# A graph kernel's second sort and sums: both chunks packed densely, items of two tiles, and ScalarE's source one-hots

## What is computed

```
agg  = jax.ops.segment_sum(x[nbr], dst, num_segments=n)      # here x is xn; "dst" is edge_index[0] = src
cnt  = jax.ops.segment_sum(jnp.ones((nbr.shape[0],), x.dtype), dst, num_segments=n)
mean = agg / jnp.maximum(cnt, 1.0)[:, None]
gnn  = x @ W1.T + b1 + mean @ W2.T + b2
...
x = x + gnn(xn) + mix(xn)          # mix: per head of 32, kv = k^T v / N with normalised k, v; out = q kv + xn
x = x + ffn(_layernorm(x))         # top-1 of 8 experts, capacity 977, 256 -> 1024 -> 256
```

## Time and profile before

| | us |
|---|---|
| median of 3 runs | 1998.8 (1995.85 to 1999.64) |
| the profiled execution's own time | 1998.75 |
| its span | 1997.1 |
| stage until the first gather | 305 |
| gathers of chunk one, 392 | 531.5 |
| gathers of chunk two, 438 | 577.4 |
| last gather to the end of the span | 583 |

### The profile page before, as it was taken

How to read it: one execution, slowest core, us unless ns; L and a number is a source line. 1 busy time by engine, 2 the same in 40 slices (tenths; PEclk the granted TensorE clock), 3 DMA queues, 4 the chain that set the end, 5 groups by cost and what they waited for, 6 DMA issues and landing times. The chain is left out here.

```text
span 1997.1 us, 27369 instructions
## 1 busy us (share of the span) xinstructions
PE 1529.7 (77%) x6558; PEld 885.3 (44%) x6558; DVE 1367.3 (68%) x3735; ACT 710.2 (36%) x1954; POOL 985.5 (49%) x969
## 2 busy tenths in 40 slices
PE   4599995667778777365665558798593999999997
PEld 2255542233333333133333335454482766666665
DVE  8998997889998988476666657666781433444344
ACT  4488890008787876000000002111281222222221
POOL 0000006777777777777777777777263111111111
PEclk7699997679999998555555558878655999999999
DMA  6980013333333333743333334444464123323200
GB/s 185 180 151 32 32 36 86 98 100 94 99 98 97 95 96 98 86 123 100 101 100 101 98 111 131 127 132 127 140 226 163 41 96 97 105 96 103 101 9 5
DMA packets 101500, 204.49 MB, mean 102 GB/s; under 512 B 19794, under 2 KB 64760, under 8 KB 99392
## 3 DMA queue, kind: packets, MB, share of 16 engines
q0 software_dynamic: 49488, 131.52, 23.6%
q1 hardware_dynamic: 43164, 64.16, 12.1%
q10 hardware_dynamic: 8700, 7.07, 1.2%
HBM read 157.43 MB, written 49.89 MB: 104 GB/s over the span
## 5 line engine op out<-in xcount | busy, mean ns | idle before, releaser
L511 POOL DMA_INDIRECT w<-xn_parts,idx x830 | 856.4, 1032 | 260.8 <-issue 236.4
L1018 DVE TENSOR_TENSOR XA<-XA,bank 128x257 f32 x878 | 367.3, 418 | 280.9 <-PE bank L765 250.1
L764 PE MATMUL bank<-w,S 128*128 (+1 forms) x878 | 294.0, 337 | 275.0 <-SPq L461 114.6
L764 PEld LDWEIGHTS bank<-w,S 128*128 128x128 f16 x878 | 93.4, 106 | 486.8 <-issue 301.1
L765 PE MATMUL bank<-w,S 128*128 (+1 forms) x878 | 298.2, 342 | 0.0
L1800 POOL DMA_INDIRECT out<-ob,tok x64 | 66.5, 1040 | 401.2 <-DVE ob L1786 384.9
L596 ACT ACTIVATE LV<-LH,v 125x128 f16<-125x128 f16 x600 | 182.5, 388 | 195.8 <-DVE LH L1268 195.5
L1724 PE MATMUL bank<-w,ht 128*117 128x256 f32 (+1 forms) x1024 | 223.7, 379 | 0.0
L1713 PE MATMUL bank<-xt,w 128*128 128x468 f32 (+1 forms) x512 | 214.8, 578 | 0.8 <-ACT xt L1738 0.8
L1748 ACT ACTIVATE ht<-bank,b1c 128x468 f32<-128x468 f32 (+1 forms) x128 | 85.6, 669 | 333.4 <-PE bank L1713 333.4
L1724 PEld LDWEIGHTS bank<-w,ht 128*117 128x117 f32 (+1 forms) x1024 | 188.8, 186 | 30.5 <-issue 0.4
(11 more groups left out here) (290 smaller groups left out, 2326.0 us busy)
## 6 DMA issues: line engine op xcount, KB each, us to landing
w<-f SPq DMA_DIRECT2D x16, 1024.0 KB, 7.6
w<-xn_parts,idx POOLq DMA_INDIRECT x830, 2.8
expert_rows<-XA SPq DMA_DIRECT2D x2, 6296.5 KB, 62.7
xb<-expert_rows SPq DMA_DIRECT2D x8, 1028.0 KB, 11.4
xb<-expert_rows SPq DMA_DIRECT2D x8, 939.7 KB
XA<-x SPq DMA_DIRECT2D x6, 1024.0 KB, 5.6
xn_parts<-w POOLq DMA_DIRECT2D x12, 512.0 KB, 3.3
work<-x ACTq DMA_DIRECT2D x48, 128.0 KB, 2.2
```

Of the source, the lines that this page charges most:

```text
L511: pool.indirect_dma_start(ring[:, o:o + 2 * D], None, tab, bass.IndirectOffsetOnAxis(ap=idx[:, t:t + 1], axis=0)).then_inc(s_g[t % RING], 16)
L764: pe.matmul(psA[t % AR][:, 0:AGW], lhs, ring_high[:, ds(o, AGW)], start=True, stop=True)
L1018: v.tensor_tensor(XA[:, ds(o, AGW)], XA[:, ds(o, AGW)], psA[t % AR][:, 0:AGW], ALU.add).then_inc(s_ev, 1)
```

## The change

1. **Chunk one becomes dense too.** Its 392 tiles become 344; `place` and `decode` go, `place_dense` and `decode_dense` serve both chunks. So the tile one-hots of chunk one are 344 wide instead of 392.
2. **An item is a pair of tiles and a block.** Two neighbouring tiles ("a two") are summed into one PSUM bank by four matmuls and added once. There are 172 and 219 twos, 220 and 267 items: 487 adds instead of 878, and 974 halves of items (each two matmuls) instead of 878 tiles.
3. **TensorE takes slots from registers in both chunks**, SyncE tells it of landed twos and lets twos go in both, and GpSimd waits for `s_free` in both.
4. **The steps are halves of items**: 440 in chunk one, 534 in chunk two. The side plan is spread over `STEPS0 - GR - SB` = 416 of 440. Heads and `own` keep their step numbers (`own` from step 288).
5. **ScalarE makes chunk two's `S`.** VectorE leaves the negated sources in 32-bit; ScalarE makes |iota - source| for 8 tiles (8 ACTIVATEs of 128) and then relu(1 - that) in one ACTIVATE of 1024, 67 times. Heads, `own` and the one-hots are interleaved on ScalarE. VectorE's 61 `source_onehots` of chunk two go; chunk one has 55 instead of 49.

```diff
-    for cols, padded in ((352, True), (448, False)):
-        tiles = (cols * EP + NB * (P - 1)) // P if padded else -(-cols * EP // P)
+    for cols in (352, 448):
+        tiles = -(-cols * EP // P)
...
+DENSE = tuple(-(-c[1] * EP // (2 * P)) * 2 for c in CHUNKS)
+TWOS = tuple(n // 2 for n in DENSE)
+ITEMS = tuple(n + NB - 1 for n in TWOS)
...
+STEPS0, STEPS1 = 2 * ITEMS[0], 2 * ITEMS[1]
...
-        while k < len(costs) and spent < total * (t + 1) // (T0 - RING):
+        while k < len(costs) and spent < total * (t + 1) // (STEPS0 - GR - SB):
...
+        for two in range(sum(TWOS)):
...
+            landed(two)
+            if AHEAD <= two < sum(TWOS) - RING // 2 + AHEAD:
+                let_go(two - AHEAD)
...
-            if t >= RING and t % 2 == 0:
-                if t < T0 + RING:
-                    pool.wait_ge(s_tile, t + 2 - RING)
-                else:
-                    pool.wait_ge(s_free, t - T0 + 2 - RING)
+            if u >= RING and u % 2 == 0:
+                pool.wait_ge(s_free, (u + 2 - RING) // 2)
...
+        def distances(j, half):
+
+            if j >= S1_GROUPS:
+                return
+            if half == 0 and j:
+                act.wait_ge(s_S1, j)
+            for n in range(half * SB // 2, (half + 1) * SB // 2):
+                ins = act.activation(far[:, n * P:(n + 1) * P], iota_1[:, :], ACT.Abs,
+                                     bias=less_src[:, j * SB + n:j * SB + n + 1])
+            ins.then_inc(s_far, 1)
+
+        def onehots(j):
+
+            if j >= S1_GROUPS:
+                return
+            act.wait_ge(s_far, 2 * j + 2)
+            act.wait_ge(s_tile, T0 + (j - 1) * SI)
+            o = (T0 // SI + j) * SB % SR * P
+            act.activation(S[:, o:o + SB * P], far, ACT.Relu, bias=ones[:, 0:1], scale=-1.0).then_inc(s_S1, 1)
...
+            for r in range(LD):
+                if HEAD0 <= g < KV_AT and r < 2:
+                    (squares, roots)[r](m, nb)
+                b = (g - OWN0) * LD + r
+                if g >= OWN0 and b < NB:
+                    own(b, b % 2)
...
+                distances(2 * g + 2 + r // 2, r % 2)
+                if r % 2:
+                    onehots(2 * g + 2 + r // 2)
...
+            if h == 0:
...
+                pe.wait_ge(s_land, item[1][i % GR] & 1023)
+                if i % SI == 0:
+                    pe.wait_ge(s_S1 if c else s_S, i // SI + 1)
+                if t >= AR:
+                    pe.wait_ge(s_ev, t - AR + 1)
+            o = item[0][i % GR]
+            lhs = S[:, q % SR * P:(q % SR + 1) * P]
+            pe.matmul(psA[t % AR][:, 0:AGW], lhs, ring_high[h][:, ds(o, AGW)], start=(h == 0), stop=True,
+                      skip_group_check=(h == 1))
+            ins = pe.matmul(psA[t % AR][:, 0:D], lhs, ring_low[h][:, ds(o, D)], start=False, stop=True, skip_group_check=True)
+            if h == 1:
+                ins.then_inc(s_tile, 1)
...
-            if t in (0, T0):
+            if t == 0:
                 source_onehots(t)
-            if t % SB == SB // 2 and t + SB // 2 not in (T0, T0 + IW):
-                source_onehots(t + SB // 2)
+            if t % SI == SI // 2 and t + SI // 2 < T0:
+                source_onehots(t + SI // 2)
...
-        for t in range(T0):
-            tile(t)
-            while ran < SIDE[t]:
+        for q in range(STEPS0):
+            if q % 2 == 0:
+                item_sum(q // 2)
+            while ran < SIDE[q]:
```

More of the change, by code:

```diff
@@ L461, in _, with let_go @@
             sp.sem_inc(s_land, 1)
-            u = t - T0 - AHEAD
-            if 0 <= u < DENSE - RING:
-                if u % GR == 0:
-                    last[:] = nc.values_load_multi_w_load_instructions(
-                        tile_used[:, u:u + GR], engines=[mybir.EngineType.SP], min_val=T0 + 1, max_val=T0 + ITEMS,
-                        skip_runtime_bounds_check_because="a tile is in no more than NB items, the place step counts them")[1]
-                sp.wait_ge(s_tile, last[u % GR] & 1023)
-                sp.sem_inc(s_free, 1)
+        def let_go(two):
+            c = two >= TWOS[0]
+            i = two - c * TWOS[0]
+            if i == 0:
+                sp.wait_ge(s_rows, c + 1)
+            if i % GR == 0:
+                many = min(GR, TWOS[c] - i)
+                last[:] = nc.values_load_multi_w_load_instructions(
+                    two_used[c][:, i:i + many], engines=[mybir.EngineType.SP], min_val=1, max_val=sum(ITEMS),
+                    skip_runtime_bounds_check_because="two tiles are in no more than NB items, the place step counts them")[1]
+            sp.wait_ge(s_tile, last[i % GR] & 1023)
+            sp.sem_inc(s_free, 1)
@@ L613, in again @@
             act.dma_start(xr[b % LD][0:rows, :], x[b * P:b * P + rows, :]).then_inc(s_xr[b % LD], 16)
-        for b in range(2):
-            again(b)
         def own(b, h):
@@ L751, in sum_tile @@
                 if i % GR == 0:
-                    many = min(GR, ITEMS - i)
+                    many = min(GR, ITEMS[c] - i)
                     item[:] = [nc.values_load_multi_w_load_instructions(
                         row[:, i:i + many], engines=[mybir.EngineType.PE], min_val=low, max_val=high,
-                        skip_runtime_bounds_check_because="an item's tile is one of the DENSE tiles, its slot one of the ring")[1]
-                        for row, low, high in ((item_slot, 0, (RING - 1) * GW), (item_need, 1, DENSE))]
@@ L757, in sum_tile @@
-                o = item[0][i % GR]
-                pe.wait_ge(s_land, item[1][i % GR] & 511)
-            if t % SB == 0:
-                pe.wait_ge(s_S, t // SB + 1)
-            if t >= AR:
-                pe.wait_ge(s_ev, t - AR + 1)
-            lhs = S[:, t % SR * P:(t % SR + 1) * P]
-            pe.matmul(psA[t % AR][:, 0:AGW], lhs, ring_high[:, ds(o, AGW)], start=True, stop=True)
-            pe.matmul(psA[t % AR][:, 0:D], lhs, ring[:, ds(o, D)], start=False, stop=True, skip_group_check=True).then_inc(s_tile, 1)
+                        skip_runtime_bounds_check_because="an item's tiles are two of its chunk's, its slots two of the ring")[1]
@@ L1217, in _ @@
         wait()
-        place(psP, psQ)
+        for _ in place_dense(0, psP, psQ):
+            pass
         after_rank = {2: lambda: pair_stats(2), 9: lambda: pair_scale(2), 14: lambda: pair_stats(3), 21: lambda: pair_scale(3),
@@ L1249, in _ @@
                 ins.then_inc(s_ht, 1)
-        decode(0)
+        for _ in decode_dense(0, 0):
+            pass
         def second_chunk():
```

373 lines of the change are left out of this document (180 added, 193 removed).

## The result

The changed kernel takes 1946.3 us (median of four runs, 1945.1 to 1947.9) beside 1998.1 us of the kernel before: a ratio of 0.974, 95% interval 0.973 to 0.975. That is faster by 52 us. The prediction said 1916, with 1904 to 1942 as its range; the gain is 30 us smaller than forecast and the time lies 4 us outside.

What follows compares the result with a forecast made beforehand. GpSimd's gathers, 1.25 us each plus excess, were taken as the bound: 307.6 + 472.4 + 549.5 = 1329.5 us at their end against 1414.0, -84.5; with 1.5 us allowed for waits, 1998.75 - 83 = 1916, range 1904 to 1942.

Steps and rivals of the forecast that it cites:

- Up to the first gather: Start of the kernel: placing costs 4.5 us more, the first sort 2 less, so the first gather comes at 307.6 us.
- 55 x 0.46 = 25.3 for `S`: Chunk one's gathers: each of VectorE's 55 `S` instructions lengthens gathers by 0.46 us, 25.3 us in all.
- 17.1 of other work, which stays: Chunk one's gathers: 17.1 us of their excess over 0.95 us each comes from VectorE's other work and remains.
- Chunk two's relief, "the 28.2 us. I keep 2 of it": Chunk two's gathers: with VectorE's 61 `S` gone, the 28.2 us of excess go but for 2, saving 26 us.
- the 15 us that I had worked out by it: Chunk two's gathers: excess kept if VectorE's other two-input instructions hold them too, by busy time; total 1931 us.
- The wait in `own`, 1.2 us for two blocks: In `own`: ScalarE's next block copy queues behind its ACTIVATE of 1024, so TensorE waits 1.2 us every two blocks.
- Late by 26 us ... The ring holds ... 40 us ... Cost 0: End of `own`: TensorE is 26 us late, the ring of 32 gathers covers 40 us, so GpSimd loses nothing.
- this as a rival: In `own`: TensorE and ScalarE wait for each other at the lower clock, costing 48 us: 1964 us, chance 0.08.
- Addressed sums in chunk one: Rival: register-addressed sums cost TensorE 0.76 us each in chunk one, 334 us more: about 2169 us, chance 0.04.
- late sort of chunk two: Rival: chunk two's sort, with 18 us in hand, ends too late for its gathers, +13 us: 1929 us, chance 0.14.
- ScalarE in chunk two: Second gather stage: making the one-hots of `S` there keeps ScalarE busy for about 285 us.
- long gathers: Rival: other work than `S` lengthens gathers, so up to 26 us stay: 1931 to 1942 us, chance 0.14.

Runs made afterwards that it cites:

- e6: The changed kernel with ScalarE's copy ahead of its one-hots, and chunk one's `S` as eight one-input `tensor_scalar` of 128 in a row: 1924.1 us.
- e10: The changed kernel with ScalarE's copy ahead, chunk one's `S` made per item and chunk two's lane one-hots by column, both as one-input `tensor_scalar`: 1935.6 us.
- e7: e6 with the lane one-hots of chunk two's sort also as one-input `tensor_scalar`, four of 128 for one of 512: 1922.3 us.

## Why the prediction was wrong, step by step

- **Up to the first gather**: 307.6 said, 308.35 measured; the sum from the earlier trace rows held.
- **Counts and beat**: 344 and 438 gathers at 1.25 us. Right, and the bulk of the gain: 48 x 1.25 = 60 us.
- **"55 x 0.46 = 25.3 for `S`"**: this failed: it is chunk one's term, and it was mis-sized. `S` held gathers for 34.6 us, 0.63 each. The 0.46 came from giving all of stage two's 28.2 us to `S`; the count gives it 20.3 of them, 0.33 each, and most of the rest to the heads. In stage one before it was 26.4 / 49 = 0.54. So the price ran from 0.33 to 0.63 by phase and by what ran ahead, and the prediction took it for a constant.
- **"17.1 of other work, which stays"**: 18.8 us after, near the number, but by luck, since it wasn't a thing that stays: it was 13.3 before. During the same 112 lane one-hots 43 gathers began before and 56 after. At a beat of 1.25 us some 112 x 0.68 / 1.25 = 61 would start within one if they fell at random, so it was before that they fell well.
- **Chunk two's relief, "the 28.2 us. I keep 2 of it"**: 6.0 are left, most of them holds by the instructions of the heads and `own` with two SBUF inputs. The forecast is off by 4 us only, though its ground, that all 28.2 were the doing of `S`, was off by 8. The rule of the Trainium skill ("GPSIMD Engine Reference", Specifications) weighed there was right in kind; the 15 us that I had worked out by it were too many.
- **The wait in `own`, 1.2 us for two blocks**: mechanism, place and size right.
- **"Late by 26 us ... The ring holds ... 40 us ... Cost 0"**: this failed, and it is the largest term. A block took 4.83 us, not 4.65: TensorE was busy for 4.16 of it where the prediction took 4.05 (the granted clock was 0.73, and the estimate rested on the 0.81 of the earlier trace rows), and idle for 0.67 where it took 0.6. Late by 48 x (4.83 - 4.12) = 34 us in all, where the ring's 40 looked like enough. It wasn't, since the ring wasn't empty of work at the start: at 1110 us, where `own` begins, GpSimd had issued 593 gathers and the adds stood at item 144 of 267, about the 580th, so 13 gathers or 16 us were in use. At 1276 us TensorE was some 24 us late, and the 40 were gone. The standstill was 13.2 us, and it began there, at the 725th gather, before the halves behind `own` could help. The prediction named this as a rival, but priced it at the lower clock throughout (1964) and put nothing between 0 and 48.
- **Addressed sums in chunk one, late sort of chunk two**: neither showed in the changed kernel. The decode was done 11 us before its 345th gather was due, where the prediction gave 18 us. The late sort did show in e6 to e10, with 9 to 15 us, once GpSimd was held less.
- **ScalarE in chunk two**: 286.8 us busy for the 285 said.
- **The range** had the two failures one at a time: 26 us for long gathers, 13 for a late stage. Both came, 12.6 and 18.7 us.

## What to carry to other kernels

A stall that comes from two engines' beats meeting has a price by phase, not by count: take it at random phase (here, as an estimate from the holds counted above, (1.22 - 0.1)^2 / (2 x 1.25) = 0.50 us an `S`, (0.68 - 0.1)^2 / 2.5 = 0.13 a lane one-hot) and keep the worst phase (1.25 measured) in the range, and don't count as fixed what another beat will move. In this case random phase gives 55 x 0.50 + 112 x 0.13 = 42 us for chunk one, which is what the prediction had, against 52 measured: it is the range that needs the phase. When a wait is put on an engine that has just enough time, don't count a buffer's full depth as cover, and ask whether a short instruction queued behind the long one can go ahead of it; here that order alone was worth 15 us. And when work is moved off an engine because it disturbs a neighbour, try another form of it where it is: short pieces gave the same relief. When a bottleneck is relieved, look at once at the next: here chunk one's sums and sort had a pace of 470 us ready behind the 485 of the gathers, and forms of `S` that freed GpSimd of 35 to 45 us (e6, e7) gained 7 to 9 us, until the sort went faster too.

## What the runs showed of the hardware

- An indirect gather issued by GpSimd is held by a running `tensor_tensor` with two SBUF inputs for the time it has left less some 0.13 us, up to 1.05 us, and up to 1.25 us where a tile one-hot ran just ahead of it. A `tensor_scalar` of 440 f16 elements (0.33 us, one SBUF input) holds it to the same rule, by 0.1 us. It isn't held by a reduction with one input of 0.95 us, nor by an add with one input in PSUM. I had expected the effect of `S`, not that the lane one-hots have it to the same rule.
- In `own` the granted clock was 0.73 with the copy behind the one-hots, TensorE busy 199.7 us for 770 matmuls, and 0.92 with the copy ahead, TensorE busy 159.7 us for 769. It idled 32.3 and 32.2 us. So the granted clock differed by a quarter at the same work and the same idle time in sum; what decided it, no run shows.
- Eight `tensor_scalar` of 128 take 1.38 us where one `tensor_tensor` of 1024 takes 1.21: cutting up costs VectorE 14%. Made two at a time, the `S` of chunk one cost it 90 us rather than 66, and that paid best.
